# Adding spread terms in PSUM and moving a one-hot column to ScalarE in the two attentions of a four-network graph kernel

## The chip, the cores and the metric

The kernel runs on 1 core of one Trainium2 chip. The metric is the device time of one execution in microseconds (us), as the median of several runs. The core's engines are named as in the profile: PE is TensorE (PEld its weight loads), DVE is VectorE, ACT is ScalarE, POOL is GpSimd and SP is SyncE. They run side by side, each in its own order, and wait for each other by semaphores.

## The reference

The input is a graph of 3125 nodes with 256 features each and 53125 edges, sorted by destination. Four graph networks follow each other, each with a residual sum and a layer norm. The change touches the first two, which are attentions over the incoming edges of each node. Cut to what matters, the second one is:

```python
score = alpha_src[src] + alpha_dst[dst]                # per edge and head
score = jnp.where(score > 0, score, 0.2 * score)
smax = jax.ops.segment_max(score, dst, num_segments=N)
ex = jnp.exp(score - smax[dst])
denom = jax.ops.segment_sum(ex, dst, num_segments=N)
msg = (ex / denom[dst])[:, :, None] * val[src]
h = jax.ops.segment_sum(msg, dst, num_segments=N)
```

The first attention has the same form with 8 heads, and its score is a dot product of a row of the source with a row of the destination. The third and the fourth network (sums over neighbours and matrix products) are not touched.

## The kernel before

Both attentions are made by one function, `attend_edges`, called with layer 0 and layer 1. The edges lie in 416 chunks of 128 (one edge a partition), and 8 chunks (G) make a group, so there are 52 groups (NG), one a tick. Each engine has its own program, a plain list of steps written out by hand, and within a tick the engines work on neighbouring groups.

**POOL** gathers the rows of the source nodes, 8 indirect DMAs a group (line 827), into a ring of four groups (RING); it may overwrite a chunk when PE has summed the chunk that stood there four groups earlier (`chunk_summed`). **SP** loads for every chunk a window of 128 destination rows (line 807). In the second attention such a row holds 24 bf16 numbers: the destination's term for 8 heads, split into three bf16 pieces (PIECES3) whose sum is the f32 number.

**DVE** makes the one-hots (`spot_slots`, two groups ahead): line 841 compares each edge's slot in its window with 0 to 127, and line 840 copies a 129th column that marks the last edge of the chunk. **PE** turns the one-hots (line 965, `turn_slots`), **ACT** copies them out of PSUM (line 1093, `copy_turned`), and PE multiplies them with the window, which spreads the destination's numbers over the edges (line 986, `spread_windows`). In the second attention that is one matmul a chunk with 24 columns, all 8 chunks into one stretch `raw` of the PSUM bank `turn_ps`, which also holds the turned scores and the peaks.

In `take_scores` of the second attention DVE first adds the three pieces (line 864, a reduction), then adds the source's term (line 867), then takes the leaky maximum (line 870). PE turns the scores (line 994), DVE scans them for each node's peak (lines 876 and 879), PE turns the peaks back (line 1000), DVE subtracts them (lines 889 and 892, `shift_scores`), ACT takes the exponential twice (lines 1100 and 1101, `weigh`), and DVE weighs the gathered rows with it in the next tick (line 897). Before `shift_scores` DVE waits for the next group's spread, as both lie in one bank.

PE then sums the weighted rows of each chunk by the one-hots (lines 1016 and 1018, `sum_parts`) into three PSUM banks in turn; the 129th column gives the sums over the node that a chunk leaves open. ACT copies each bank to SBUF, 128 columns in line 1119 and the ends in line 1121 (`copy_sums`); PE may fill a bank again when that is done (`evacuated`).

The second attention also counts the edges into an adjacency matrix for the third network: DVE makes two more one-hots a tick (lines 929 and 931), PE multiplies them (line 1031), ACT copies the counts (line 1134), and SP stores them in 16 parts (line 795).

The orders of PE and ACT within a tick are the functions `tick_rows` (first attention) and `tick_alpha` (second).

Of the kernel before, what the change touches and what calls it, by code (L numbers as in the profile page):

```python
# [6 lines left out]
F32 = mybir.dt.float32  # L7
# [3 lines left out]
ALU = mybir.AluOpType  # L11
# [3 lines left out]
P = 128  # L15
# [6 lines left out]
H = 8  # L22
DK = D // H
RING = 4
# [681 lines left out]
def attend_edges(nc, keep, layer, by_src, by_part, ws, wd, scale, adj=None, begun=None):  # L706
# [7 lines left out]
    with Phase(nc) as ctx:  # L714
        def sb(name, shape, dt):
            return ctx.enter_context(nc.sbuf_tensor(f"e{layer}_" + name, shape, dt))
        from_src = begun["rows"] if begun else sb("from_src", [P, RING, G, ws], F32)
        window = sb("window", [P, 2, G, wd], by_part.dtype)
        raw_score = sb("raw_score", [P, 2, G * H], F32) if layer else None
        spread_score = sb("spread_score", [P, 2, G * H], F32) if layer else None  # L720
        score = sb("score", [P, 2, G * H], F32)
        shifted = sb("shifted", [P, 2, G * H], F32)
        peak = sb("peak", [G * H, 2, P], F32)
# [33 lines left out]
        part_ps = [pst(f"part_ps{i}") for i in range(BANKS)]  # L757
        hot_ps = pst("hot_ps", BF16, G * P)
        spread_ps = [turn_ps] if layer else [pst(f"spread_ps{i}") for i in range(2)]
        raw = turn_ps[:, P + G * H:P + G * H + G * wd] if layer else None  # L760
        count_ps = [pst(f"count_ps{i}") for i in range(2 if counting else 0)]
        (scored, t_turned, fwd, peaked, t_back, shift_done, prob, prob_kept, mask_done, weighted,
         zeroed, slots_set, ident_set, pe_passed, hot, hot_turned, hot_copied) = sems(
# [2 lines left out]
                "prob", "prob_kept", "mask_done", "weighted", "zeroed", "slots_set", "ident_set", "pe_passed", "hot", "hot_turned",  # L766
                "hot_copied")))
        chunk_summed = sems(nc, ctx, *(f"e{layer}_chunk_summed{b}" for b in range(RING)))
        evacuated, raw_made = sems(nc, ctx, f"e{layer}_evacuated", f"e{layer}_raw_made")
        LANDED = 1 if layer else PAIRS  # L770
        src_in = begun["rows_in"] if begun else [sems(nc, ctx, *(f"e{layer}_src_in{b}_{i}" for i in range(LANDED))) for b in range(RING)]
        win_in = sems(nc, ctx, *(f"e{layer}_win_in{b}" for b in range(2)))
# [59 lines left out]
        def _(v):  # L832
# [4 lines left out]
            def spot_slots(g):  # L837
                it, b = g // RING, g % RING
                v.wait_ge(chunk_summed[b], G * it + 1)
                nc.vector.tensor_copy(onehot[:, b, :, P], keep["last"][:, bass.ds((RING * it + b) * G, G)]).then_inc(hot, 1)  # L840
                nc.vector.tensor_tensor(onehot[:, b, :, 0:P], slots.unsqueeze(1).to_broadcast([P, G, P]),
                                        keep["slot"][:, bass.ds((RING * it + b) * G, G)].unsqueeze(2).to_broadcast([P, G, P]),
                                        ALU.is_equal).then_inc(hot, 1)
# [9 lines left out]
            def take_scores(g):  # L853
                it, b, r = g // RING, g % RING, g % 2
                if layer == 0:
                    for i in range(2):
                        v.wait_ge(used[i], PAIRS // 2 * (g + 1) + 1)
                    nc.vector.tensor_reduce(score[:, r, :].rearrange("p (j h) -> p j h", h=H),
                                            from_src[:, b, :, D:2 * D].rearrange("p j (h d) -> p j h d", h=H),
                                            AX_X, ALU.add).then_inc(scored, 1)  # L860
                else:
                    v.wait_ge(src_in[b][0], 16 * G * it + 16 * G)
                    v.wait_ge(spread[r], g // 2 + 1)
                    nc.vector.tensor_reduce(spread_score[:, r, :].rearrange("p (j h) -> p j h", h=H),
                                            raw.rearrange("p (j c h) -> p j h c", c=PIECES3, h=H), AX_X, ALU.add).then_inc(used[r], 1)
                    v.wait_ge(used[r], g // 2 + 2)
                    nc.vector.tensor_tensor(raw_score[:, r, :].rearrange("p (j h) -> p j h", h=H), from_src[:, b, :, D:D + H],
                                            spread_score[:, r, :].rearrange("p (j h) -> p j h", h=H), ALU.add).then_inc(raw_made, 1)
                    v.wait_ge(raw_made, g + 1)
                    nc.vector.scalar_tensor_tensor(out=score[:, r, :], in0=raw_score[:, r, :], scalar=0.2,  # L870
                                                   in1=raw_score[:, r, :], op0=ALU.mult, op1=ALU.max).then_inc(scored, 1)
# [77 lines left out]
        def _(pe):  # L949
# [6 lines left out]

            def turn_slots(g):
                b = g % RING
                pe.wait_ge(hot, 2 * (g + 1))
                pe.wait_ge(hot_copied, g + 1)  # L960
                pe.sem_inc(pe_passed, 1)
                for j in range(G):

                    upper = onehot[:, b, j, 0:P].bitcast(BF16)[:, 1::2]
                    mm = nc.tensor.transpose(hot_ps[:, j * P:(j + 1) * P], upper, ident16[:, :])
                mm.then_inc(hot_turned, 1)

            def spread_windows(g, chunks):
                r, pair = g % 2, g // 2

                if chunks[0] == 0:
                    pe.wait_ge(win_in[r], 16 * G * pair + 16 * G)
                    pe.wait_ge(hot_copied, g + 2)
                for j in chunks:
                    if layer == 0:
                        s = j // 2 % 2
                        if j % 2 == 0:
                            pe.wait_ge(used[s], PAIRS // 2 * g + j // 4 + 1)
                        to = spread_ps[s][:, j % 2 * D:(j % 2 + 1) * D]
                    else:  # L980
                        s = r
                        if j == 0:

                            pe.wait_ge(used[1 - s], pair + 1 + s)
                        to = raw[:, j * wd:(j + 1) * wd]
                    mm = nc.tensor.matmul(to, onehot_t[:, r, j, :], window[:, r, j, :], start=True, stop=True)  # L986
                    if (layer == 0 and j % 2) or j == G - 1:
                        mm.then_inc(spread[s], 1)
# [13 lines left out]
            def sum_parts(g, chunks):  # L1002
                if g < 0:
                    return
                b, r = g % RING, g % 2
                if chunks[0] == 0:
                    pe.wait_ge(weighted, g + 1)
                    pe.wait_ge(mask_done, g + 1)
                    pe.wait_ge(prob_kept, g + 1)
# [77 lines left out]
        def _(act):  # L1087
            act.sem_inc(hot_copied, 1)

            def copy_turned(g):  # L1090
# [2 lines left out]
                nc.scalar.activation(onehot_t[:, r, :, :], hot_ps[:, :].rearrange("p (j e) -> p j e", j=G),  # L1093
                                     ACT.Copy).then_inc(hot_copied, 1)

            def weigh(g):
                r = g % 2
                act.wait_ge(shift_done, g + 1)
                by_head = shifted[:, r, :].rearrange("p (j h) -> p j h", h=H)
                nc.scalar.activation(share(r), by_head, ACT.Exp, scale=scale).then_inc(prob, 1)  # L1100
                nc.scalar.activation(small[:, r, :, 0:H], by_head, ACT.Exp, scale=scale).then_inc(prob_kept, 1)
# [33 lines left out]

            def tick_rows(g):
                copy_sums(g - 2, range(4, G))
                copy_sums(g - 1, (0, 1, 2))
                if g + 2 < NG:
                    copy_turned(g + 2)  # L1140
                weigh(g)
                copy_sums(g - 1, (3,))

            def tick_alpha(g):
                copy_sums(g - 2, range(4, G))
                copy_counts(g - 1, 0, 1)
                copy_sums(g - 1, (0, 1))
                copy_counts(g - 1, 1, 2)
# [8 lines left out]
            def clear_sums(k):  # L1157
                nc.scalar.activation(keep["sums"][:, k, :], keep["once"][:, C:C + 1].to_broadcast([P, PBUF]),
                                     ACT.Copy).then_inc(cleared, 1)

            clear_sums(0)
            copy_turned(0)
            copy_turned(1)
# [1986 lines left out]
```

## Time and profile before

| what | us |
|---|---|
| median of three runs | 2908.68 |
| the three runs | 2904.08, 2908.68, 2914.31 |
| the profiled execution's own time | 2904.07 |
| its span on the core | 2902.3 |
| first attention: first gather issued, last one issued | 132.69, 652.75 |
| second attention: first gather issued, last one issued | 820.17, 1337.86 |
| TensorE clock granted, mean | 0.957 of full speed |

The span is the time between the first and the last instruction of the program in the profiled execution. Times in rows are counted from its start. A row of the timeline gives the start, the duration, the engine, the line of the kernel, the operation, what it writes and reads, and in square brackets how long the engine sat idle before and what ended that. A name such as e_turn_ps is a buffer of the program; the name x in the first attention is the room in which its one-hots lie.

### The profile page before, as it was taken

How to read it: one execution, taken by the hardware profiler on the slowest of the kernel's cores; microseconds unless marked ns; L12 is line 12 of the kernel's file. 1: busy time of each engine (PE TensorE's matmuls, PEld its weight loads, DVE VectorE, ACT ScalarE, POOL GpSimd, SP SyncE). 2: the span in 40 equal slices, each digit the busy share in tenths (PEclk: the TensorE clock that was granted, in tenths of full speed). 3: DMA queues.
4: the chain of work that ended last, by engine and by line, in shares of the span. 5: the costliest groups of instructions: out<-in, count | busy, mean ns of one | idle time of the engine just before them, and what ended most of it. 6: DMA issues, size and time to landing. Idle time of an engine off the chain costs nothing. (4 is left out here: it accounts for less than half of the span.)

```text
span 2902.3 us, 53181 instructions
## 1 busy us (share of the span) xinstructions
PE 2627.4 (91%) x17158; PEld 1910.1 (66%) x17158; DVE 1546.9 (53%) x2779; ACT 1106.6 (38%) x3027; POOL 973.4 (34%) x1020
## 2 busy tenths in 40 slices
PE   6789999998747888877799999999999989999998
PEld 4679999996636777776455555555555566565654
DVE  8589999996457988886712414124141251111123
ACT  1145555554346777776312304023040252111111
POOL 3577777773477777773400101001010000000000
PEclk8999999999869999999799999999999999999999
DMA  7799999992348898896554342533415133434342
GB/s 261 254 320 321 315 316 318 316 313 96 99 103 142 152 151 158 154 153 107 162 163 115 105 126 63 164 113 105 133 55 165 43 127 111 140 89 132 114 122 86
DMA packets 332504, 470.20 MB, mean 162 GB/s; under 512 B 155942, under 2 KB 243062, under 8 KB 331588
## 3 DMA queue, kind: packets, MB, share of 16 engines
q1 hardware_dynamic: 269364, 286.33, 38.0%
q0 software_dynamic: 59088, 176.67, 19.9%
q10 hardware_dynamic: 3776, 3.80, 0.4%
q8 instruction: 139, 2.28, 0.3%
q14 instruction: 137, 1.12, 0.1%
HBM read 412.95 MB, written 55.50 MB: 161 GB/s over the span
## 5 line engine op out<-in xcount | busy, mean ns | idle before, releaser
L2368 PE MATMUL sum_ps<-room,high 128*128 128x391 f16 x1900 | 469.3, 330 | 2.4 <-DVE z_t L2545 2.4
L2368 PE MATMUL sum_ps<-room,low 128*128 128x391 f16 x1824 | 453.5, 330 | 0.0
L827 POOL DMA_INDIRECT e_from_src<-vk,src x416 | 394.4, 948 | 140.7 <-issue 108.9
L827 POOL DMA_INDIRECT rows<-val,src x410 | 388.8, 948 | 134.7 <-issue 102.8
L2766 PE MATMUL sum_ps<-room,high 128*128 128x391 f16 x1200 | 389.4, 329 | 0.5 <-DVE x L2910 0.5
L2766 PE MATMUL sum_ps<-room,low 128*128 128x391 f16 x1152 | 379.3, 329 | 0.0
L1016 PE MATMUL e_part_ps<-e_onehot,rows 128*128 128x129 f32 x1664 | 289.3, 298 | 77.6 <-ACT ends L1121 69.3
L2545 DVE SCALAR_TENSOR_TENSOR z_t<-h_t,own,sum_ps 128x391 f32<-128x391 f32 x80 | 44.7, 617 | 482.4 <-PE sum_ps L2368 478.7
L1016 PEld LDWEIGHTS e_part_ps<-e_onehot,rows 128*128 128x128 f32 x1664 | 226.1, 197 | 105.7 <-ACT ends L1121 94.5
L1119 ACT ACTIVATE sums<-e_part_ps 128x384 f32 x416 | 205.5, 494 | 227.9 <-PE e_part_ps L1018 201.6
L2436 POOL TENSOR_SCALAR h_t<-h_t 128x391 f32<-128x391 f32 x32 | 39.0, 1237 | 693.8 <-DVE h_t L2575 693.8
L1016 PE MATMUL e_part_ps<-x,e_from_src 128*128 128x129 f32 x1664 | 267.0, 283 | 1.7 <-DVE e_from_src L897 1.2
L2368 PEld LDWEIGHTS sum_ps<-room,high 128*128 128x128 f16 x1900 | 184.9, 98 | 125.9 <-issue 3.0
L2368 PEld LDWEIGHTS sum_ps<-room,low 128*128 128x128 f16 x1824 | 177.9, 98 | 127.1 <-issue 1.6
L2445 ACT ACTIVATE gin_y_t<-gin_proj_ps,gin_columns 128x391 f32<-128x391 f32 x80 | 47.0, 588 | 559.7 <-PE gin_proj_ps L2385 558.9
L1119 ACT ACTIVATE room<-e_part_ps 128x384 f32 x416 | 206.5, 496 | 135.6 <-PE e_part_ps L1018 70.4
L1016 PEld LDWEIGHTS e_part_ps<-x,e_from_src 128*128 128x128 f32 x1664 | 229.7, 191 | 20.0 <-DVE e_from_src L897 2.1
L986 PE MATMUL e_spread_ps<-e_window,x 128*128 128x256 f32 x832 | 214.6, 385 | 14.9 <-DMA e_window<-q_part 14.8
L2766 PEld LDWEIGHTS sum_ps<-room,high 128*128 128x128 f16 x1200 | 116.8, 97 | 80.3 <-issue 1.2
L986 PEld LDWEIGHTS e_spread_ps<-e_window,x 128*128 128x128 f32 x832 | 144.5, 193 | 33.5 <-DMA e_window<-q_part 12.4
L850 DVE TENSOR_TENSOR e_from_src<-e_from_src,e_spread_ps 128x512 f32<-128x512 f32 x208 | 139.6, 671 | 49.2 <-PE e_spread_ps L986 47.3
L2766 PEld LDWEIGHTS sum_ps<-room,low 128*128 128x128 f16 x1152 | 112.3, 97 | 80.4 <-issue 2.1
(424 smaller groups left out, 4558.3 us busy)
## 6 DMA issues: line engine op xcount, KB each, us to landing
room<-adj SPq DMA_DIRECT2D x128, 977.5 KB, 4.9
e_window<-q_part SPq DMA_DIRECT2D x416, 128.0 KB
room<-adj SPq DMA_DIRECT2D x32, 488.8 KB
room<-adj SPq DMA_DIRECT2D x32, 391.0 KB
adj<-e_counts SPq DMA_DIRECT2D x8, 1250.0 KB
adj<-e_counts SPq DMA_DIRECT2D x8, 1193.8 KB
e_from_src<-vk,src POOLq DMA_INDIRECT x416, 4.5
rows<-val,src POOLq DMA_INDIRECT x416
```

The source lines that it names most:

```text
L827: nc.gpsimd.indirect_dma_start(from_src[:, b, j, :], None, by_src, bass.IndirectOffsetOnAxis(ap=keep["src"][:, g * G + j:g * G + j + 1], a ...
L850: nc.vector.tensor_tensor(k_rows, k_rows, spread_ps[pair % 2][:, :].rearrange("p (j d) -> p j d", j=2), ALU.mult).then_inc(used[pair % 2], 1)
L986: mm = nc.tensor.matmul(to, onehot_t[:, r, j, :], window[:, r, j, :], start=True, stop=True)
L1016: nc.tensor.matmul(part_ps[s][:, k * ENDS:(k + 1) * ENDS], from_src[:, b, j, k * P:(k + 1) * P], onehot[:, b, j, :], start=True, stop=True)
L1119: nc.scalar.activation(keep["sums"][:, :, bass.ds(starts[j], P)], of[:, :, 0:P], ACT.Copy).then_inc(whole_copied, 1)
L2368: mm = nc.tensor.matmul(sum_ps[KH * n + m][:, 0:AN], part[:, t, m * P:(m + 1) * P], slab[s][:, n, k * AN:(k + 1) * AN], start=(t == 0 and ...
L2436: nc.gpsimd.tensor_scalar(h_t[:, 1, cols(b)], h_t[:, 1, cols(b)], 0.0, None, ALU.max).then_inc(floored, 1)
L2445: nc.scalar.activation((z_t if p else y_t)[:, m, cols(b)], proj_bank(p, v)[:, 0:AN], ACT.Identity, bias=columns[:, 3 * p, m:m + 1], scale= ...
L2545: nc.vector.scalar_tensor_tensor(out=z_t[:, m, cols(b)], in0=h_t[:, m, cols(b)], scalar=own[:, l:l + 1], in1=sum_ps[KH * n + m][:, 0:AN], ...
L2766: mm = nc.tensor.matmul(sum_ps[KH * n + m][:, 0:AN], part[:, t, m * P:(m + 1) * P], slab[s][:, n, k * AN:(k + 1) * AN], start=(t == 0 and ...
```

## The change

In the second attention PE no longer writes 24 columns a chunk. It makes three matmuls of 8 columns, with the same turned one-hots as weights and one piece of the window each, that accumulate into the same 8 columns of PSUM. `raw` shrinks from 192 to 64 columns, and DVE's reduction (line 864) goes away with the buffer it wrote; the addition of the source's term reads `raw` from PSUM itself. PE's wait for the reduction before a new spread becomes a wait for the scores of the group before.

In both attentions the column of last edges is written by ACT (`mark_last`), right after ACT has copied chunks 4 to 7 of the group that used the buffer before, and for the first two groups ahead of ACT's first step. Its wait is for the sums of that group, its semaphore is `last_marked`, and PE waits for it before the sums of a group. `hot` counts one step a group instead of two.

```diff
             def spot_slots(g):
                 v.wait_ge(chunk_summed[b], G * it + 1)
-                nc.vector.tensor_copy(onehot[:, b, :, P], keep["last"][:, bass.ds((RING * it + b) * G, G)]).then_inc(hot, 1)
                 nc.vector.tensor_tensor(onehot[:, b, :, 0:P], ...).then_inc(hot, 1)
...
                     v.wait_ge(spread[r], g // 2 + 1)
-                    nc.vector.tensor_reduce(spread_score[:, r, :].rearrange("p (j h) -> p j h", h=H),
-                                            raw.rearrange("p (j c h) -> p j h c", c=PIECES3, h=H), AX_X, ALU.add).then_inc(used[r], 1)
-                    v.wait_ge(used[r], g // 2 + 2)
                     nc.vector.tensor_tensor(raw_score[:, r, :].rearrange("p (j h) -> p j h", h=H), from_src[:, b, :, D:D + H],
-                                            spread_score[:, r, :].rearrange("p (j h) -> p j h", h=H), ALU.add).then_inc(raw_made, 1)
+                                            raw.rearrange("p (j h) -> p j h", h=H), ALU.add).then_inc(raw_made, 1)
...
             def turn_slots(g):
-                pe.wait_ge(hot, 2 * (g + 1))
+                pe.wait_ge(hot, g + 1)
...
                     else:
                         s = r
-                        if j == 0:
-
-                            pe.wait_ge(used[1 - s], pair + 1 + s)
-                        to = raw[:, j * wd:(j + 1) * wd]
+                        if g and j == 0:
+                            pe.wait_ge(scored, g)
+                        for c in range(PIECES3):
+                            mm = nc.tensor.matmul(raw[:, j * H:(j + 1) * H], onehot_t[:, r, j, :], window[:, r, j, c * H:(c + 1) * H],
+                                                  start=(c == 0), stop=(c == PIECES3 - 1))
+                        if j == G - 1:
+                            mm.then_inc(spread[s], 1)
+                        continue
...
             def sum_parts(g, chunks):
                 if chunks[0] == 0:
+                    pe.wait_ge(last_marked, g + 1)
                     pe.wait_ge(weighted, g + 1)
...
+            def mark_last(g):
+                if g >= RING:
+                    act.wait_ge(chunk_summed[g % RING], G * (g // RING) + 1)
+                nc.scalar.activation(onehot[:, g % RING, :, P], keep["last"][:, g * G:(g + 1) * G], ACT.Copy).then_inc(last_marked, 1)
...
             def tick_rows(g):
                 copy_sums(g - 2, range(4, G))
+                if g + 2 < NG:
+                    mark_last(g + 2)
                 copy_sums(g - 1, (0, 1, 2))
...
             def tick_alpha(g):
                 copy_sums(g - 2, range(4, G))
+                if g + 2 < NG:
+                    mark_last(g + 2)
                 copy_counts(g - 1, 0, 1)
...
+            mark_last(0)
+            mark_last(1)
             clear_sums(0)
```

## Rows read from the trace of the kernel before

**Rows 1.** Windows, both attentions: us, busy time by engine (instructions), PEclk, DMA share.

```profile
150.00:650.00 500.00, 492.45 (x3628) 446.66 (x3628) 457.59 (x602) 272.41 (x921) 378.32 (x399) 1.00 0.95 318
930.00:1330.00 400.00, 329.43 (x3157) 294.23 (x3158) 349.68 (x483) 298.49 (x893) 302.73 (x320) 0.98 0.90 155
```

**Rows 2.** Page's groups, second attention's gathers: busy us, mean ns | idle before.

```profile
L827 POOL DMA_INDIRECT rows<-val,src x410 | 388.8, 948 | 134.7 <-issue 102.8
```

**Rows 3.** Timeline of POOL: start, us, what [idle before]; first and last gather.

```profile
820.17 0.95 POOL L827 DMA_INDIRECT rows<-val,src  x1 [4.89 <-POOLq L79]
...
1337.86 0.94 POOL L827 DMA_INDIRECT rows<-val,src  x1 [0.31 <-issue]
```

**Rows 4.** Timeline of POOL, its three gathers that waited in the second attention.

```profile
917.45 0.95 POOL L827 DMA_INDIRECT rows<-val,src  x1 [3.63 <-PE e_part_ps L1018]
920.12 0.94 POOL L827 DMA_INDIRECT rows<-val,src  x1 [1.72 <-PE e_part_ps L1018]
921.73 0.95 POOL L827 DMA_INDIRECT rows<-val,src  x1 [0.66 <-PE e_part_ps L1018]
```

**Rows 5.** Timeline of DVE, one tick of the second attention from scan to scan.

```profile
963.33 0.42 DVE L876 TENSOR_TENSOR_SCAN e_fixed<-link,e_turn_ps 64x128 f32<-64x128 bf16 x1 [0.16 <-PE e_turn_ps L994]
964.13 0.14 DVE L840 CAST e_onehot<-last 128x8 f32<-128x8 bf16 x1
964.18 1.21 DVE L841 TENSOR_TENSOR e_onehot<-e_fixed,slot 128x1024 f32<-128x1024 f32 x1
965.31 1.74 DVE L929 TENSOR_TENSOR e_is_place<-e_fixed,place_t 128x1536 f16<-128x1536 f32 x1
...
968.87 0.34 DVE L864 TENSOR_REDUCE e_spread_score<-e_turn_ps 128x64 f32<-128x192 f32 x1
969.24 0.23 DVE L867 TENSOR_TENSOR e_raw_score<-rows,e_spread_score 128x64 f32<-128x64 f32 x1
...
972.63 0.42 DVE L876 TENSOR_TENSOR_SCAN e_fixed<-link,e_turn_ps 64x128 f32<-64x128 bf16 x1 [0.71 <-PE e_turn_ps L994]
```

**Rows 6.** Waits, 930 to 1330 us: who waited for whom: us, times, longest us.

```profile
DVE e_fixed L876 <- PE e_turn_ps L994: 29.4, 30, 3.0
DVE e_spread_score L864 <- DMA rows<-val,src: 11.5, 11, 2.3
PE e_part_ps L1016 <- ACT ends L1121: 56.5, 73, 2.4
```

**Rows 7.** Timeline of DVE, first attention: the scans of groups 12 and 23.

```profile
277.68 0.41 DVE L876 TENSOR_TENSOR_SCAN e_fixed<-link,e_turn_ps 64x128 f32<-64x128 bf16 x1
...
387.03 0.41 DVE L876 TENSOR_TENSOR_SCAN e_fixed<-link,e_turn_ps 64x128 f32<-64x128 bf16 x1
```

**Rows 8.** Waits of DVE, 150 to 650 us.

```profile
DVE e_from_src L850 <- PE e_spread_ps L986: 34.3, 50, 2.5
```

**Rows 9.** Timeline of PE, two spreads of eight chunks in the second attention.

```profile
915.30 0.39 PE L986 MATMUL e_turn_ps<-e_window,e_onehot_t 128*128 128x24 bf16 x8 [8.35 <-DMA e_window<-alpha_part]
...
964.53 0.36 PE L986 MATMUL e_turn_ps<-e_window,e_onehot_t 128*128 128x24 bf16 x8
```

**Rows 10.** By line, L986 and L1789: duration ns min/median/max, first, last start.

```profile
L986 PE MATMUL e_turn_ps<-e_window,e_onehot_t x416: 172/173/202, 829.6 to 1347.3; 128*128 128x24 bf16 x139
...
L1789 PEld LDWEIGHTS n_alpha_ps<-w_all,x_t x100: 190/192/337, 754.8 to 794.2; 128*128 128x128 f32 x100
```

**Rows 11.** Timeline of ACT, second attention, behind a group's last copied chunk.

```profile
973.52 0.17 ACT L1121 ACTIVATE ends<-e_part_ps 128x6 f32<-128x6 f32 x1
973.58 0.68 ACT L1134 ACTIVATE e_counts<-e_count_ps,whole 128x500 f16<-128x500 f32 x1
```

**Rows 12.** Waits of PE's weight loads, 820 to 1380 us.

```profile
PEld e_turn_ps L1000 <- issue: 16.4, 52, 1.3
```

**Rows 13.** Timelines of POOL and DVE between the two attentions.

```profile
814.33 0.95 POOL L1676 DMA_INDIRECT rows<-val,src  x1 [0.30 <-issue]
...
819.57 0.29 DVE L833 COPY e_fixed<-iota 128x128 f32<-128x128 f32 x1 [9.18 <-PEq L79]
```

More of the change, by code:

```diff
@@ L719, in attend_edges @@
         raw_score = sb("raw_score", [P, 2, G * H], F32) if layer else None
-        spread_score = sb("spread_score", [P, 2, G * H], F32) if layer else None
         score = sb("score", [P, 2, G * H], F32)
@@ L759, in attend_edges @@
         spread_ps = [turn_ps] if layer else [pst(f"spread_ps{i}") for i in range(2)]
-        raw = turn_ps[:, P + G * H:P + G * H + G * wd] if layer else None
+        raw = turn_ps[:, P + G * H:P + 2 * G * H] if layer else None
         count_ps = [pst(f"count_ps{i}") for i in range(2 if counting else 0)]
@@ L768, in attend_edges @@
         chunk_summed = sems(nc, ctx, *(f"e{layer}_chunk_summed{b}" for b in range(RING)))
-        evacuated, raw_made = sems(nc, ctx, f"e{layer}_evacuated", f"e{layer}_raw_made")
+        evacuated, raw_made, last_marked = sems(nc, ctx, *(f"e{layer}_{n}" for n in ("evacuated", "raw_made", "last_marked")))
         LANDED = 1 if layer else PAIRS
```

## The prediction

> **What bounds the kernel now.** The change touches only the two attention stages, each 52 ticks of one group of 1024 edges, so I read the page's slices to place them (150 to 650 and 930 to 1330 us are inside them), then the busy time of each engine there [rows 1]. In the first attention PE is busy 492 of 500 us, DVE 458, ACT 272. In the second nobody is full: of 400 us DVE has 350, PE 329, POOL 303, ACT 298. Busy shares alone would name DVE there. They mislead, because POOL's 76% is a full queue: a gather takes 948 ns and the next starts 0.3 us after its end [rows 2].
>
> So I read POOL in order of time. In the second attention its first gather starts at 820.17 and its last, the 410th, at 1337.86 [rows 3]: 517.69 us. Three of the 409 steps hold a wait beyond the usual 0.30 us, 3.33 + 1.42 + 0.36 = 5.11 us, all at 917 to 922 us [rows 4]. The rest is (517.69 - 5.11) / 409 = 1.253 us a gather, 10.03 us a group. Nothing that DVE, ACT or PE do holds POOL up outside that one place. The others' tick is shorter when nothing disturbs it: from scan to scan 972.63 - 963.33 = 9.30 us [rows 5]. They then run into rows that have not landed: DVE's first step of a tick waits for a gather 11 times, 11.5 us, all in this stretch [rows 6]. **The second attention goes at the pace of the gathers**, and its other engines have about 11.5 / 52 = 0.22 us a tick to spare.
>
> The first attention is different. Its scans stand 387.03 - 277.68 = 109.35 us apart over 11 ticks, 9.94 us each [rows 7], a little under POOL's 10.03, with PE at 98.5% [rows 1]; DVE waits 34.3 us for PE's spread there [rows 8]. **The first attention goes at PE's pace.** The late stages, over half of the span, are not touched.
>
> **The change part by part.** The sum is made against the profiled execution's own 2904.07 us (span 2902.3 and 1.77 around it), which lies 4.61 under the median 2908.68 of the three runs and at the lower end of them.
>
> *Scores of the second attention.* DVE loses the reduction of the three pieces (L864). Its cost on DVE's own path runs from its start to the next one's, 969.24 - 968.87 = 0.37 us [rows 5]. The addition that follows reads PSUM in place of SBUF; the subtraction L892 in the same tick, of the same size, already does that, so I cost it at 0. Gain on DVE: 52 x 0.37 = 19.2 us. Behind it stands DVE's weighing of the rows, then a wait for PE's turned scores, which ended the idle time before 30 scans, 29.4 us in all [rows 6]; in the tick shown DVE sits 0.71 us idle there [rows 5]. So most of the 0.37 becomes more of that wait, and what is not swallowed becomes more of the wait for rows. On the end of the stage: 0.
>
> *PE's three matmuls a chunk instead of one.* 16 more weight loads and matmuls a tick, of 8 columns where 24 stood. Eight pairs took 0.36 us [rows 9], one alone shows 0.17 (L986's median) [rows 10], so a further pair costs (0.36 - 0.17) / 7 = 0.027 us, and 16 cost 0.43 us. Bounds: below, 0, since the columns in sum are the same; above, the nearest row of 8 columns, the f32 matmul L1789: its load takes 192 ns [rows 10], 16 x 0.192 = 3.1 us. I take 0.43: same line, type and weights. Who waits: DVE's shift (L889) waits for this spread, but before it DVE runs two comparisons, from 965.31 to about 968.6 in the tick shown [rows 5], while PE starts the spread at 964.53 [rows 9] and has over 3 us to spare; PE itself idles 56.5 us in those 400 waiting for ACT [rows 6], 1.4 us a tick. Covered, except at one place. At 915.30 the spread is late because its windows are [rows 9], and the sums that release POOL's three late gathers come right behind it on PE. There 0.43 us goes straight onto POOL's queue. The eight pairs took 0.39 us there, hardly more. **Term: +0.4**, bounds 0 and +3.1.
>
> Against this price stands a rule. In the rows, eight pairs fit in 0.36 us [rows 9]. The Trainium skill, "TensorE: Matmul & The Clock Gate", section "Back-to-back issue gap", gives about 81 ns a matmul for a stream of load and matmul pairs of 128 columns. By it the sixteen would be an estimated 1.3 us and the term +1.3; the trace's 27 ns decides for this shape.
>
> *ScalarE's column of last edges.* DVE loses a small copy (L840), but the next instruction starts 964.18 - 964.13 = 0.05 us after it [rows 5], so only 0.05 a tick is won on its path, 2.6 us in each attention, swallowed like the rest. ACT gains one 128x8 copy a tick. Nearest row: the copy of the ends, 128x6, 0.17 us, whose successor starts 0.06 after it [rows 11]. Bounds: 0.06 and 0.17; I take 0.1, as the copy of counts follows directly here too. Its wait (all chunks of group g - 2 summed) is met: ACT has just copied the last of those. Queued behind it on ACT are the copy of counts, the copies that free PE's banks and the exponentials, for which DVE's weighing waits. So it moves ACT's chain by 0.1 us, half of the 0.22 to spare: 0 on the end of the second attention. In the first, ACT is busy 54% [rows 1] and waits for PE: 0.
>
> *Waits.* In the sums PE gains a wait for last_marked, set two ticks earlier; in the spread the wait for "scored" replaces one and is met by the turn of scores just before. I cost both at 0; if such a wait ever stood open it would hold PE's sums. Bounds: 0, and an issue gap like the one before the turn of peaks, 16.4 us over 52 ticks [rows 12], in each attention. Nearest is 0: the sums already begin with three such waits.
>
> *Head and tail.* Before group 0 ACT writes two columns, 0.34 us at most [rows 11], where PE still waits for its first windows. In the drain after the last gather DVE's saving counts once or twice, and the longer spread takes as much: 0.
>
> Sum: 0 + 0.4 + 0 + 0 = +0.4: 2904.5 for the profiled execution, 2909.1 for the median. **Forecast 2909, no measurable change.**
>
> **The rivals.** *Faster: DVE sets the second attention's pace.* For it: DVE has the highest share there [rows 1]. Against it: POOL's unbroken queue [rows 3, 4]. Price: 52 x (0.37 + 0.05) = 21.8, and 2.6 in the first attention, so 24.4 at most: about 2885. It decides if POOL turns out to follow the others by its ring of four groups; a half gain lies at 2897.
>
> A variant is that the gathers themselves get shorter. In the gap between the stages DVE is idle for 9.18 us until 819.57, and the gather at 814.33 still takes 0.95 us [rows 13], as all 410 do on the mean [rows 2]. The Trainium skill, "DMA: Bandwidth & Descriptors", section "SWDGE vs HWDGE vs iDMA", says that GpSimd's descriptor rings are SBUF state which DVE can lock it out of. By that rule less DVE work would shorten the queue; by this row it has nothing to give back, so I add only a little chance. Its price, at most DVE's freed time, is the same 22 us.
>
> *Slower: PE and ACT set the pace.* PE's 0.43 and ACT's 0.17 on the path would be 0.60 a tick; 52 x 0.60 = 31.2 less the 11.5 of waits for rows that it would first eat gives +19.7: about 2928. It decides once the two add more than 0.22 us a tick on the chain copy of sums, PE's sums, turned scores. For it: PE waits 56.5 us for ACT [rows 6], so ACT's chain leads PE's and whatever lengthens it is handed on. Against it: the spread lies beside 3 us of comparisons. Its neighbour is PE's new wait: at 16.4 us in each attention [rows 12] it gives 33 at most, and half of that 2925.
>
> *The edit does not free DVE:* if the score addition on PSUM cost what the reduction did, nothing would move, since what it frees is swallowed anyway: 2909 again.
>
> **How the numbers follow.** Forecast 0.67 (2909; its own range 2901 to 2917, as the three runs span 5 us to either side), DVE's pace 0.16 and shorter gathers 0.02 (2885 to 2898), slower 0.14 (2918 to 2929), edit without effect 0.01. The upper half of the faster cases and most of the slower ones make the range 2889 to 2923. Under 0.3% (8.7 us) this kernel cannot be told from no change: faster 0.18, same 0.68, slower 0.14.
>
> **What would show it.** Right: in the second attention DVE's busy time falls by about 25 us, L864 is gone, DVE's waits before the scan and for rows grow by about as much; POOL's first to last gather stays at 518 us within 2; the 24 matmuls of a tick take some 0.8 us; ACT has 52 more copies of 0.15 us in each stage; the first attention's ticks stay at 9.94. Wrong: gathers closer than 10.03 us a group, or new POOL waits beyond 0.3 us after 930 us (slower), or a first attention whose ticks leave 9.94.

## The result and the profile after

The changed kernel takes 2921.26 us (median of 14 runs), the kernel before, run beside it, 2907.86 us (14 runs). The ratio is 1.0048, 95% interval 1.0037 to 1.0059, so 11 to 17 us **slower**. This is inside the range of the prediction, but its main forecast, no measurable change, is wrong. One run of the kernel before (2968.74 us) and one of e10 below (9355.53 us) lie far from all others and are left out of the ratios. All differences below are such ratios times 2909 us, each against the kernel before in the same series, whose median goes from 2907.86 to 2912.17 us between the series. The 95% interval stands in brackets: the change costs +14.0 [10.8, 17.2].

The first fence is the view of busy time by engine after, in the stretches of [rows 1], with the same columns.

```profile
150.00:650.00 500.00, 493.23 (x3618) 446.66 (x3618) 453.02 (x550) 277.02 (x968) 378.07 (x401) 1.00 0.95 318
930.00:1330.00 400.00, 339.59 (x3632) 306.56 (x3630) 321.81 (x384) 287.75 (x896) 291.48 (x308) 0.94 0.89 151
```

The edits do what they say. In the second attention DVE is busy 321.81 us in place of 349.68, PE has 475 matmuls more and is busy 10 us more. But POOL's gathers in the same 400 us fall from 320 to 308, so less work passes through: the stage is slower. PE's granted clock there is 0.94 after 0.98. In the first attention the numbers stay, and so does its tick, 9.96 us after 9.94 [rows 7]: (388.54 - 278.99) / 11 in this timeline of DVE.

```profile
278.99 0.41 DVE L871 TENSOR_TENSOR_SCAN e_fixed<-link,e_turn_ps 64x128 f32<-64x128 bf16 x1
...
388.54 0.41 DVE L871 TENSOR_TENSOR_SCAN e_fixed<-link,e_turn_ps 64x128 f32<-64x128 bf16 x1
```

So the loss whose place is clear lies in the second attention. POOL's timeline after, first gather, one of its stalls, last gather:

```profile
823.65 0.95 POOL L826 DMA_INDIRECT rows<-val,src  x1 [4.77 <-POOLq L79]
...
952.64 0.95 POOL L826 DMA_INDIRECT rows<-val,src  x1 [3.92 <-PE e_part_ps L1018]
955.31 0.95 POOL L826 DMA_INDIRECT rows<-val,src  x1 [1.72 <-PE e_part_ps L1018]
957.13 0.94 POOL L826 DMA_INDIRECT rows<-val,src  x1 [0.87 <-PE e_part_ps L1018]
...
1352.30 0.95 POOL L826 DMA_INDIRECT rows<-val,src  x1 [0.31 <-issue]
```

First to last gather takes 1352.30 - 823.65 = 528.65 us after 517.69 [rows 3], 10.96 more. That is most of the 17.9 us between the two profiled spans (2920.2 and 2902.3). Some 3.5 us lie ahead of the first gather and 3.5 behind the last one, but these two stretches also vary without the change: the first gather stands at 820.17 us in before, the earliest of all 14 profiles, and at 828.00 in e5 below, which is faster. The gather itself is no longer, 0.95 us, nor the 0.30 us between two. What is new are waits for PE's sums: 15 of over 0.35 us, 16.9 us beyond the usual 0.30 in all, where before had three with 5.1 [rows 4]. Why PE's sums come late there is in PE's timeline just before, and a tick later:

```profile
945.80 0.24 PE L999 MATMUL e_turn_ps<-ident,e_peak 64*128 64x64 f32 x1
950.06 0.80 PE L980 MATMUL e_turn_ps<-e_window,e_onehot_t 128*128 128x8 bf16 x24 [4.02 <-DMA e_window<-alpha_part]
950.73 1.21 PE L1016 MATMUL e_part_ps<-e_onehot,rows 128*128 128x129 f32 x4
...
961.24 0.76 PE L980 MATMUL e_turn_ps<-e_window,e_onehot_t 128*128 128x8 bf16 x24
```

A window of destination rows is missing, PE stands for 4.02 us, and the sums stand behind the spread in its queue. When it goes on, four matmuls of the sums take 1.21 us, where they took 0.71 at 942.43 us. The granted clock tells why: after PE stood it was at 0.50, the lower of its two levels (1.2 of 2.4 GHz), for this stretch (columns as in [rows 1]), and at 1.00 from 957 to 967 us.

```profile
950.10:956.60 6.50, 6.50 (x58) 6.35 (x59) 0.88 (x5) 3.57 (x9) 1.90 (x2) 0.50 0.15 28
```

So a late window costs its own wait and then some slow sums. The stall before at 915 us [rows 9] is of the same kind; after has more of them that reach POOL. The waits after, 930 to 1330 us (us in all, times, longest):

```profile
DVE e_fixed L871 <- PE e_turn_ps L993: 36.7, 34, 3.8
PE e_part_ps L1016 <- ACT ends L1126: 36.2, 57, 2.2
DVE rows L892 <- ACT e_fixed L1105: 26.8, 17, 4.7
PE e_turn_ps L980 <- DMA e_window<-alpha_part: 14.3, 8, 5.1
DVE e_raw_score L862 <- DMA rows<-val,src: 6.4, 6, 1.9
```

Against [rows 6], DVE waits less for gathered rows (11.5 to 6.4 us) and more for PE (29.4 to 36.7): the gathers are less often what comes last. An undisturbed tick has even become a little shorter, 1010.01 - 1000.76 = 9.25 us after 9.30 [rows 5]. This timeline of DVE shows it, with the addition that now reads PSUM:

```profile
1000.76 0.42 DVE L871 TENSOR_TENSOR_SCAN e_fixed<-link,e_turn_ps 64x128 f32<-64x128 bf16 x1 [0.91 <-PE e_turn_ps L993]
...
1006.22 0.20 DVE L862 TENSOR_TENSOR e_raw_score<-rows,e_turn_ps 128x64 f32<-128x64 f32 x1
...
1010.01 0.42 DVE L871 TENSOR_TENSOR_SCAN e_fixed<-link,e_turn_ps 64x128 f32<-64x128 bf16 x1 [0.80 <-PE e_turn_ps L993]
```

So not the tick grew; stalls did. The windows come from SP, a queue that the prediction had not read. SP's timeline before: a row is a group's eight issues, from the first one's start to the last one's end. The gap to the next row is SP loading the next group's eight starts into registers, one instruction each.

```profile
824.07 4.03 SPq L807 DMA_DIRECT2D e_window<-alpha_part  x8
832.71 3.99 SPq L807 DMA_DIRECT2D e_window<-alpha_part  x8
...
1039.06 3.94 SPq L807 DMA_DIRECT2D e_window<-alpha_part  x8
1043.04 0.56 SPq L795 DMA_DIRECT2D adj<-e_counts  x1
1050.78 5.47 SPq L807 DMA_DIRECT2D e_window<-alpha_part  x8
...
1334.15 4.69 SPq L807 DMA_DIRECT2D e_window<-alpha_part  x8
```

A plain group takes SP 832.71 - 824.07 = 8.64 us, one with a store of counts 1050.78 - 1039.06 = 11.72. From the first group to the last it is (1334.15 - 824.07) / 51 = 10.00 us a group, and no wait of SP for PE is among the waits of this stage, in either kernel. **SP's queue is as full as POOL's**, which needs 10.03. After, SP's timeline gives (1347.99 - 827.56) / 51 = 10.20 us a group, though nothing of SP was edited:

```profile
827.56 4.01 SPq L806 DMA_DIRECT2D e_window<-alpha_part  x8
...
1159.32 6.65 SPq L806 DMA_DIRECT2D e_window<-alpha_part  x8
...
1347.99 4.84 SPq L806 DMA_DIRECT2D e_window<-alpha_part  x8
```

From first to last issue within a group, added over the 52 groups, before has 207 us and after 216; the gaps between groups stay, 307 and 309 us. So the issuing grew, as in the middle row, where eight issues took 6.65 us.

SP's windows thus take (1347.99 - 827.56) - (1334.15 - 824.07) = 10.35 us longer, nearly the 10.96 by which the gathers grew. As SP does not wait for PE, a longer spread on PE cannot have held SP up through any wait. Nor is the spread's own time enough: PE waits for a window 13 times in the second attention after, and 13 x 0.40 us, the time that the 16 pairs add (below), is 5.2 us at most.

Which windows come late is not chance either. SP's timeline after shows what went ahead of the window that was missing at 950 us:

```profile
927.94 1.46 SPq L794 DMA_DIRECT2D adj<-e_counts  x1
936.35 4.84 SPq L806 DMA_DIRECT2D e_window<-alpha_part  x8
```

The group's last issue ends at 941.19, but PE can go on only at 950.06, 8.87 us later. The group stands right behind a store of counts. By the trace's semaphore events the 15 groups behind a store land 4.3 to 9.7 us after their last issue ends (median 7.9), the other 37 within 3.4 us (median 1.8); before it is 6.6 to 11.3 and within 3.5. Apart from the first three groups, each window for which PE waits, before and after, is one behind a store. So SP's full queue leaves no lead, and the windows behind the stores are those that then come too late.

### The profile page after: what moved, and what is told of

Its sections match the earlier page's. It is cut to its first block and busy times, and to the rows that moved or that the text cites. A ratio compares the mean times of both kernels' runs of the same rounds, so it can differ in the third digit from the quotient of the medians.

```text
span 2920.2 us, 54792 instructions
## 1 busy us (share of the span) xinstructions
PE 2661.0 (91%) x17990; PEld 1942.2 (67%) x17990; DVE 1523.9 (52%) x2623; ACT 1115.5 (38%) x3131; POOL 970.0 (33%) x1020
## 5 line engine op out<-in xcount | busy, mean ns | idle before, releaser
L2379 PEld LDWEIGHTS sum_ps<-room,low 128*128 128x128 f16 x1824 | 178.0, 98 | 127.2 <-issue 1.8
L1018 PE MATMUL e_part_ps<-e_onehot,e_small 128*65 128x129 f32 x832 | 166.6, 283 | 0.0
L985 PEld LDWEIGHTS e_spread_ps<-e_window,x 128*128 128x128 f32 x832 | 144.4, 193 | 33.3 <-DMA e_window<-q_part 11.5
```

The lines of the kernel that those rows point to most:

```text
L1018: nc.tensor.matmul(part_ps[s][0:SMALL, KH * ENDS:(KH + 1) * ENDS], small[:, r, j, :], onehot[:, b, j, :], start=True, stop=True).then_inc( ...
L2379: mm = nc.tensor.matmul(sum_ps[KH * n + m][:, 0:AN], part[:, t, m * P:(m + 1) * P], slab[s][:, n, k * AN:(k + 1) * AN], start=(t == 0 and ...
```

## The experiments

| kernel | median, us | ratio to before [95%] | us |
|---|---|---|---|
| changed kernel | 2921.26 | 1.0048 [1.0037, 1.0059] | +14.0 |
| e1: PSUM half only | 2920.78 | 1.0040 [1.0025, 1.0054] | +11.6 |
| e2: ScalarE half only | 2914.17 | 1.0010 [0.9999, 1.0021] | +2.9 |
| e3: 24 matmuls, DVE as before | 2924.08 | 1.0056 [1.0041, 1.0072] | +16.3 |
| e4: 8 matmuls, no reduction | 2913.45 | 1.0007 [0.9996, 1.0018] | +2.0 |
| e5: before, SP with half the loads | 2901.05 | 0.9967 [0.9955, 0.9979] | -9.6 |
| e6: changed, SP with half the loads | 2904.50 | 0.9978 [0.9965, 0.9992] | -6.4 |
| e7: two wide matmuls more | 2914.93 | 1.0021 [1.0002, 1.0040] | +6.1 |
| e8: before, one load of eight | 2897.82 | 0.9969 [0.9958, 0.9981] | -9.0 |
| e9: changed, one load of eight | 2905.45 | 0.9996 [0.9982, 1.0010] | -1.2 |
| e10: 16 pairs more, elsewhere | 2912.76 | 1.0020 [1.0003, 1.0038] | +5.8 |
| e11: e8 and the PSUM half | 2904.70 | 0.9979 [0.9964, 0.9993] | -6.1 |
| e12: e8 with fewer POOL waits | 2902.03 | 0.9968 [0.9955, 0.9981] | -9.3 |

### Which half costs: e1 to e4

The theories of this first series blame PE's 16 more pairs of weight load and matmul, ACT's new copy, or what DVE's shorter step sets off earlier.

**e1_psum_only** has the PSUM half of the change alone; the mark of last edges stays on DVE.

```diff
-                        to = raw[:, j * wd:(j + 1) * wd]
+                        for c in range(PIECES3):
+                            mm = nc.tensor.matmul(raw[:, j * H:(j + 1) * H], onehot_t[:, r, j, :], window[:, r, j, c * H:(c + 1) * H],
+                                                  start=(c == 0), stop=(c == PIECES3 - 1))
...
```

> The kernel before with the three accumulating matmuls alone; DVE still copies the column of last edges. The changed kernel was 13 us slower than before. Theory PE (the 16 more loads and matmuls a tick cost the second attention): about +13 us. Theory ACT (the new copy on ScalarE lengthens the chain that leads): 0. Theory early (a freed DVE brings PE sooner to windows that have not landed, PE stands, and POOL then waits for its sums): +10 or more, as most of DVE's gain comes from this part.

Measured +11.6 [7.3, 15.7]: most of the loss.

**e2_mark_only** has ACT's `mark_last` alone.

```diff
+                nc.scalar.activation(onehot[:, g % RING, :, P], keep["last"][:, g * G:(g + 1) * G], ACT.Copy).then_inc(last_marked, 1)
...
```

> The kernel before with ScalarE writing the column of last edges in both attentions; the scores as before. Theory PE: 0. Theory ACT: about +13 us, with POOL's waits in the second attention up from 5 to some 15 us. Theory early: 0 to +2, as DVE is freed by only 0.05 us a tick on its path.

Measured +2.9 [-0.3, 6.1]: at most a small part, not told from 0 here.

**e3_pe_24** makes 24 matmuls of 8 columns, each into its own columns, and DVE reduces them as before: PE's cost without DVE's gain.

```diff
-                        to = raw[:, j * wd:(j + 1) * wd]
+                        for c in range(PIECES3):
+                            at = j * wd + c * H
+                            mm = nc.tensor.matmul(raw[:, at:at + H], onehot_t[:, r, j, :], window[:, r, j, c * H:(c + 1) * H],
+                                                  start=True, stop=True)
...
```

> The kernel before with 24 matmuls of 8 columns a tick instead of 8 of 24, each into its own columns; DVE still adds the pieces. So PE has the new instructions and DVE no gain. Theory PE: +13 us. Theory ACT: 0. Theory early: 0 to +2, since nothing on DVE gets shorter.

Measured +16.3 [11.9, 20.9]: the pairs alone cost all of it.

**e4_dve_only** makes one matmul of 8 columns a chunk and no reduction; pieces two and three are left out of the scores. That is DVE's gain without PE's pairs.

```diff
-                        for c in range(PIECES3):
+                        for c in range(1):
...
```

> The kernel before with one matmul of 8 columns a chunk and no reduction: it leaves out the second and third piece of the destination's term, so PE has no new instructions and DVE has the whole gain of 0.37 us a tick. Theory PE: 0 or a few us faster. Theory ACT: 0. Theory early: +10 us or more, with late windows in front of PE as in the changed kernel.

Measured +2.0 [-1.2, 5.2]: 0.37 us a tick less on DVE is worth nothing by itself, and it does no harm either. The late windows that theory early expects did come: in e4's profile PE waits for windows 16 times, 38.8 us, and POOL's waits beyond 0.30 us add up to 11.4. They did not bring the loss, so PE's wait for windows is no measure of it by itself. What follows from the four: the change costs by PE's pairs.

### Whether SP's full queue makes them cost: e5 to e7

**e5_sp_half_before** and **e6_sp_half_after** give SP time to spare, in either kernel. Half of the windows hold wrong rows, as the expectation says.

```diff
-                starts = [sp.value_load(...) for j in range(G)]
+                starts = [sp.value_load(...) for j in range(G // 2 if layer else G)]
+                starts = starts * 2 if layer else starts
```

> The kernel before, in whose second attention SP loads only four of a group's eight starts and issues windows 4 to 7 with the starts of 0 to 3 (so half the windows hold wrong rows and the output of that attention is wrong; the eight transfers stay). In the trace of before SP needs 4.9 us for eight register loads, 3.6 us and more for eight issues and some 3.2 us for each of 15 stores, and never waits: 514 us for 52 groups. Here it has some 2.45 us a group to spare. Theory POOL (the 10.03 us a group of eight gathers set the pace of before): POOL waits only 5.1 us in all, so at most 5 us faster than before. Theory SP (SP's queue sets it, at 9.9 us a group): much more, down to the undisturbed tick of 9.3 us if POOL could follow; since POOL can't, again about 5 us, but then POOL's waits must go to nearly nothing and PE's 21 us of waiting for windows too.

> The same edit on the changed kernel (half of the windows hold wrong rows). Theory PE time (the 16 more pairs lie on the path whatever SP does): it stays some 10 us above e5. Theory SP (windows come late because SP, always busy, issues them more slowly; with spare time in SP they come in time and the 16 pairs are covered): within 3 us of e5, and so some 13 to 16 us faster than the changed kernel; PE's wait for windows and POOL's waits beyond 0.30 us (16.8 us in the changed kernel) fall to under 6 us.

Measured -9.6 [-13.1, -6.1] and -6.4 [-10.2, -2.3]. With a relieved SP the same change costs 3.2 us where it cost 14.0, and the changed kernel gains 20. That is what theory SP expected; theory PE time, 10 us between the two, falls. e5 gained more than the 5 us that theory POOL allowed before: POOL was not the only full queue. PE's waits for windows over the second attention, in the kernel before:

```profile
PE e_turn_ps L986 <- DMA e_window<-alpha_part: 21.2, 11, 8.4
```

The same view of the changed kernel:

```profile
PE e_turn_ps L980 <- DMA e_window<-alpha_part: 31.3, 13, 5.7
```

The same view of e5:

```profile
PE e_turn_ps L988 <- DMA e_window<-alpha_part: 5.9, 3, 3.1
```

POOL's waits beyond 0.30 us go with them, to 1.6 us in e5 and 4.5 in e6, after 16.9 in the changed kernel.

**e7_pe_wide** adds PE time to the kernel before at the place of the pairs, in few instructions.

```diff
+                    if layer and j == G // 2:
+                        for _ in range(2):
+                            nc.tensor.matmul(turn_ps[:, P + G * H + G * wd:2 * P + G * H + G * wd], keep["ident"][:, :],
+                                             keep["ident"][:, :], start=True, stop=True)
```

> The kernel before with two matmuls more a tick among the window matmuls of the second attention (fp32, 128 columns, into columns that nobody reads): about as much time of PE as the 16 pairs (0.43 to 0.6 us) in two pairs of instructions in place of 16. Theory PE time: 10 to 16 us slower than before. Theory instructions (the number of PE's instructions, which have to be fetched, makes the time): under 3 us.

PE's timeline of e7, a spread:

```profile
1007.28 0.26 PE L990 MATMUL e_turn_ps<-e_window,e_onehot_t 128*128 128x24 bf16 x4
1007.39 0.69 PE L988 MATMUL e_turn_ps<-ident 128*128 128x128 f32 x4
1007.92 0.25 PE L990 MATMUL e_turn_ps<-e_window,e_onehot_t 128*128 128x24 bf16 x4
```

The spread takes 1008.17 - 1007.28 = 0.89 us, 0.53 more than before's 0.36 [rows 9]; the change's 24 matmuls take 0.76, 0.40 more. The cost is +6.1 [0.6, 11.6], between both theories. The kernel to set beside it is e3, which has no gain on DVE either: its 24 matmuls take 0.76 us too, so it adds less time to PE than e7 and costs more, +16.3 [11.9, 20.9] from six runs; the two intervals just miss each other. More PE time between window and sums may cost something, but it does not look like what makes the 16 short pairs dear. In the profiles SP's time goes with the cost: from its first group of windows to its last it takes 522.6 us in e3 and 509.3 in e7, after 510.08 in before.

### A version that computes the same: e8 and e9

**e8_one_load_before** and **e9_one_load_after** load a group's eight starts with one instruction.

```diff
-                starts = [sp.value_load(keep["offset"][0:1, bass.ds(g * G + j, 1)], min_val=0, max_val=PARTS) for j in range(G)]
+                if layer:
+                    _, starts = nc.values_load_multi_w_load_instructions(keep["offset"][0:1, g * G:(g + 1) * G], engines=(mybir.EngineType.SP,),
+                                                                         min_val=0, max_val=PARTS)
+                else:
+                    starts = [sp.value_load(keep["offset"][0:1, bass.ds(g * G + j, 1)], min_val=0, max_val=PARTS) for j in range(G)]
```

> The kernel before; in the second attention SP fills the eight registers of a group with one load instruction over the eight neighbouring starts, in place of eight loads of 4.9 us in all. It computes what before computes. Theory SP: SP gets time to spare as in e5 (there 2.45 us a group, 8 to 10 us faster than before with POOL's queue as the next bound), so 8 to 11 us faster, POOL's waits beyond 0.30 us under 3 us. Should one instruction for eight registers take as long as eight instructions, no change.

> The same one load of eight starts in the changed kernel; it computes what both compute. Theory SP: as e6, 14 to 18 us faster than the changed kernel, 4 to 8 us faster than before, and 2 to 5 us slower than e8. Theory PE time: 10 us or more slower than e8.

e8 takes 2897.82 us, -9.0 [-12.2, -5.5]: **faster than both kernels**. e9 has -1.2 [-5.2, 2.9], 15 us better than the changed kernel as theory SP expected, but 7.8 above e8, more than its 2 to 5 and less than the 10 of theory PE time. So relieving SP takes 6 of the 14 us off the change's cost in this pair, and 11 in e5 and e6: SP's full queue explains a part of the loss, not all of it. Where the 7.8 us lie, the profiles don't show: first to last gather is 513.41 us in e8 and 1338.04 - 824.46 = 513.58 in e9, whose profiled run, 2899.03 us, is the fastest of its twelve. SP's timeline of e8:

```profile
824.44 4.02 SPq L811 DMA_DIRECT2D e_window<-alpha_part  x8
831.26 3.95 SPq L811 DMA_DIRECT2D e_window<-alpha_part  x8
```

The waits of SP and PE in e8's second attention:

```profile
SPq L811 <- PE e_turn_ps L990: 96.2, 45, 9.4
PE e_turn_ps L990 <- DMA e_window<-alpha_part: 3.1, 1, 3.1
```

A plain group now takes SP 6.82 us in place of 8.64. SP runs ahead until it waits for PE to free a window, 96.2 us in all, and PE waits for a window once in place of 11 times. POOL's timeline of e8 shows that its queue is what is left:

```profile
822.32 0.94 POOL L831 DMA_INDIRECT rows<-val,src  x1 [4.85 <-POOLq L79]
...
1335.73 0.95 POOL L831 DMA_INDIRECT rows<-val,src  x1 [0.30 <-issue]
```

That is 513.41 us, 10.04 a group, 2.0 of it waits beyond 0.30.

### What is left: e10 to e12

**e10_pairs_parked** puts 16 pairs of 8 columns into the kernel before at another place.

```diff
-                sum_parts(g - 2, range(4, G))
+                sum_parts(g - 2, (4, 5))
+                for j in range(G if g >= 2 else 0):
+                    for _ in range(2):
+                        nc.tensor.matmul(hot_ps[:, :].bitcast(F32)[:, j * H:(j + 1) * H], onehot_t[:, g % 2, j, :],
+                                         onehot_t[:, g % 2, j, 0:H], start=True, stop=True)
+                sum_parts(g - 2, (6, 7))
```

> The kernel before with 16 pairs more a tick of the second attention, of the size of the change's (8 columns, into a PSUM bank that is overwritten later), put where PE waits for ScalarE's copies most (ahead of the sums of chunk 6: 45 us of PE's idle time, in 46 of 52 ticks). The same count of instructions as the changed kernel has, and its matmul time covered by that wait. Theory place (the pairs cost because they stand between the window and the sums): under 3 us slower than before. Theory instructions (their number costs, wherever they stand): 10 to 16 us slower, as with the 24 matmuls of 8 columns in the spread.

Measured +5.8 [0.9, 11.1], between the two theories again. The pairs took 1109.88 - 1109.47 = 0.41 us a tick in PE's timeline,

```profile
1109.47 0.55 PE L1061 MATMUL e_hot_ps<-e_onehot_t 128*128 128x8 bf16 x16
1109.88 0.69 PE L1016 MATMUL e_part_ps<-e_onehot,rows 128*128 128x129 f32 x4
```

20.5 us in 50 ticks. PE's waits for ACT's copies over the second attention, in the kernel before:

```profile
PE e_part_ps L1016 <- ACT ends L1121: 67.5, 87, 2.4
```

The same view of e10:

```profile
PE e_part_ps L1016 <- ACT ends L1126: 51.2, 73, 2.2
```

They shrank by 16.3 us, so by this sum some 4 us were not covered. But e10's profile has 1345.43 - 828.02 = 517.41 us from first to last gather, no more than before's 517.69, so where its 5.8 us lie is not shown. Against e3, with as many pairs more in the spread and no gain on DVE either, the intervals just miss each other: place matters, then, but neither place seems free.

**e11_one_load_psum** is e8 with the PSUM half, that is, with the edits of e8 and e1.

> The kernel before with the three accumulating matmuls and with SP's one load of eight starts, the mark of last edges staying on VectorE: e8 and the PSUM half of the change. e9 with both halves stood some 8 us above e8. If the 16 more pairs cost what is left, it is 5 to 8 us above e8 (3 to 6 us faster than before); if the mark on ScalarE does, within 2 us of e8 (9 to 11 us faster than before). Theory SP alone: within 2 us of e8.

Measured -6.1 [-10.5, -2.0], 2.9 us above e8, at the edge between the expected cases. With SP relieved the PSUM half costs about 3 us where it cost 11.6, and e9, with the mark on ACT too, stands 4.9 higher. Each of these differences is uncertain by some 5 us.

**e12_one_load_pool** is e8 with half of POOL's waits on PE left out.

```diff
-                    if it:
-                        pool.wait_ge(chunk_summed[b], G * (it - 1) + j + 2)
+                    if it and (layer == 0 or j % 2 == 0):
+                        pool.wait_ge(chunk_summed[b], G * (it - 1) + j + (3 if layer else 2))
```

> e8 with half of POOL's waits on PE's sums left out of the second attention (it waits once for the sums of two chunks, for the later of the two). If POOL's queue (0.95 us a gather and 0.30 us between two) is the bound once SP has time to spare, and a wait is part of the 0.30 us, it is faster than e8, by 3 us or more; if the 0.30 us are the gather's own, it is within 2 us of e8.

Measured -9.3 [-13.1, -5.5], as e8. In POOL's timeline of e12 gathers stand as close as before, with or without a wait, so the 0.30 us are the gather's own:

```profile
1105.09 0.95 POOL L831 DMA_INDIRECT rows<-val,src  x1 [0.31 <-issue]
1106.34 0.95 POOL L831 DMA_INDIRECT rows<-val,src  x1 [0.30 <-PE e_part_ps L1022]
1107.59 0.95 POOL L831 DMA_INDIRECT rows<-val,src  x1 [0.30 <-issue]
```

## Why the prediction was right and wrong

**What bounds the kernel: half right.** The first attention at PE's pace held (9.96 us a tick). "The second attention goes at the pace of the gathers" left out a second queue. SP issues its windows at 10.00 us a group without ever waiting for PE, and it was read only as something PE waits for [rows 9]. e5 and e8 gained 9 to 10 us by relieving SP alone, more than the 5.11 us that POOL's waits allowed. With two full queues the 0.22 us a tick to spare are no cover at the places where a window comes last.

**DVE's gain: right.** DVE's busy time fell by 28 us in 400, the addition on PSUM costs no more than the one on SBUF (0.20 us after 0.23 [rows 5]), and e4 shows that nothing of it reaches the end. So the rival "DVE sets the pace" falls. The variant of shorter gathers falls too, as a gather takes 0.95 us after as before.

**PE's pairs: the size right, the cover wrong.** This is the step that failed. The 16 pairs were put at 0.43 us a tick and take 0.40. The 81 ns a matmul of the Trainium skill, "TensorE: Matmul & The Clock Gate", section "Back-to-back issue gap", a figure for pairs of 128 columns, would have made it 1.3; the trace has 25 ns for this shape of 8 columns. But the term "covered, except at one place", +0.4 us, measured +11.6 [7.3, 15.7] in e1 and +16.3 in e3, far outside its bounds of 0 to +3.1. In an undisturbed tick the cover holds, as the tick of 9.25 us shows. The prediction took the late window at 915 us for the only place, an accident; it was the sign of SP's full queue and of the store ahead of that window. What the runs show in place of "covered" is this: SP's windows took 10.35 us longer, the gathers behind them 10.96, and with SP relieved the change cost 3 us (e6) or 8 (e9), its PSUM half 3 (e11). The pairs' own time in the late ticks, 5.2 us at most, does not make up the loss. How the pairs make SP's issues longer is not shown.

**ScalarE's mark: not settled.** The copy takes 0.22 us, where its nearest row had 0.17, but on ACT's path it adds only 1001.81 - 1001.71 = 0.10 us, as predicted. ACT's timeline after:

```profile
1001.65 0.17 ACT L1126 ACTIVATE ends<-e_part_ps 128x6 f32<-128x6 f32 x1
1001.71 0.22 ACT L1099 ACTIVATE e_onehot<-last 128x8 f32<-128x8 bf16 x1
1001.81 0.68 ACT L1139 ACTIVATE e_counts<-e_count_ps,whole 128x500 f16<-128x500 f32 x1
```

Its term was 0; measured +2.9 [-0.3, 6.1] in e2. With the new wait, which e2 has too, it is small at most.

**The slower rival: the sign and the size, not the mechanism.** "PE and ACT set the pace" gave 2928, and 2921 came. But it was to act in every tick, once 0.22 us were used up. The undisturbed tick got shorter, and by that rule e7's 0.53 us a tick would have cost 52 x 0.53 - 11.5 = 16 us; it cost 6. So it is luck that the measured time lies within the stated range: its upper end came from this rival. Of the signs named in the prediction, the one that came is "new POOL waits beyond 0.3 us after 930 us".

**What stays open.** Why SP, unedited, needs 10.20 us a group after in place of 10.00. In the profiles SP's windows span 525 to 527 us, first to last issue, in the three kernels with 24 small matmuls in the spread and an unrelieved SP (after, e1, e3), and 514 to 521 in before, e2, e4, e7 and e10. The growth lies mostly in single long issues: after has one of 3.03 us at 1255.62, before none above 1.61. The number of PE's instructions is an obvious suspect, as the DMA queue that the profile calls instruction carries 7 packets more of some 16 KB. Its line (packets, MB, share) before:

```profile
q8 instruction: 139, 2.28, 0.3%
```

The same line of after:

```profile
q8 instruction: 146, 2.39, 0.3%
```

But in e10 the queue carries 145 packets and SP's windows span only 517 us, so the packets alone do not do it. One profile each is thin evidence. No run moved or dropped the stores of counts, so what share of the loss hangs on the windows behind them is open too; so is what the lower clock after each stall adds.

## What to carry to other kernels

Before calling one queue the pace of a stage, work out the time per group of every in-order queue, the one that only issues DMAs and loads registers among them: it never shows as busy, and its mark is that it never waits for the buffers it fills. A cover read from an undisturbed tick is no cover in the ticks where a transfer comes last; count those ticks, and ask what makes the transfer late: here a store ahead of it in the same queue. Relieving the hidden queue by one wide register load was worth 9 us here, more than any of the arithmetic that the change moved.

## What the hardware showed that was not expected

One instruction that loads eight neighbouring values into registers made a plain group of SP 1.82 us shorter than eight single loads (6.82 us after 8.64).

A store of counts is issued in 0.56 us, but it makes SP's group 11.72 us long where a plain one has 8.64, and the windows issued right behind it land 7.9 us (median) after their last issue ends, where others take 1.7 (the kernel before).

A further pair of weight load and matmul of 8 columns took (0.76 - 0.36) / 16 = 0.025 us in a run of 24 of them, which took the place of 8 pairs of 24 columns.

After PE had stood for 4.02 us its granted clock was 0.50 for the next 6.5 us, and four matmuls that take 0.71 us at 1.00 took 1.21.
